# Hybrid layer: the next rows' transposes in the FFN moved from TensorE to VectorE blocks and device memory

## Chip, core and metric

The kernel runs on one core of one Trainium2 chip. The metric is device microseconds of a whole execution; lower is better. The core has TensorE (PE in the profile, with PEld for its weight loads), VectorE (DVE), ScalarE (ACT), GpSimd (POOL) and SyncE (SP), which here only issues DMAs. Engines wait for each other through semaphores alone.

## The reference, cut to what matters

Input `x` has 2 batches of 1024 rows of 512. Four sublayers follow each other, each added to `x`: a gated linear attention (A), an FFN (F1), a softmax attention (B) and the same FFN again (F2).

```python
def _qlinear(x, wq, scale):
    W = (wq - 128.0) * scale[:, None]
    return einsum('bsd,hd->bsh', x, W)
gate = silu(_qlinear(x, wq_gate, s_gate))            # 512 -> 1408
up   = _qlinear(x, wq_up, s_up)                      # 512 -> 1408
ffn  = _qlinear(gate * up, wq_down, s_down)          # 1408 -> 512
...
x = x + linear_attention(layernorm(x)); x = x + ffn(layernorm(x))
x = x + attention(layernorm(x));        x = x + ffn(layernorm(x))
```

## The kernel before, in words

The 2048 rows live in SBUF (`xres`), 16 tiles of 128 rows. An FFN block works on one batch (8 tiles), so there are four: F1,0 and F1,1, then B, then F2,0 and F2,1 (`blk` 0 to 3). A block has two parts.

The gate/up loop runs over `j`, the 11 slices of 128 hidden units. For each, TensorE makes seven partial products (pieces 1, 2, 7, 6, 4, 5, 3, each four matmuls of 512 columns), a scheme of seven block products on split 16-bit halves. They need the batch's normalised rows with the feature dimension on the partitions, as high and low parts of seven sums: `ab`, `12`, `34` and `2`. DVE, ACT and POOL combine the seven into `hid` and split it again. Piece 1 of `j = 0` waits for the low part of `ab`, pieces 6 and 5 for `12` low, and piece 7 for `34` low.

The down stage runs over `t`, the 8 row tiles: 11 matmuls of `hid_lo` and 11 of `hid_hi` per tile. ACT drains the low bank (`y_low`, L1233), DVE adds the high bank (`yt`, L1882), POOL scales (`yt`, L925), DVE adds to `xres` (`add_y`, L1801). The banks of `down_lo` are 6 and 2 in turn, of `down_hi` 5 and 7.

The next set of rows is prepared inside the block. A set is 8 tiles, handled as four pairs `i`. `x_stats` gives a row tile's mean and variance, `x_normalise` writes both tiles of a pair to `xn`, and TensorE turns them (`turn_x`, L2169: four 128x128 transposes for each tile, against an identity) into two PSUM banks. ACT copies the first bank to `x_first` (L1014) and makes the high parts (L1021, L1024); DVE makes `x_mid` by two subtractions (`x_second`, L1484 and L1487) and a low part (L1489); POOL makes `x_last` (`x_sums`, L753 and L755), `x_ab_low` (L761) and `x_12_low` (L767); ACT makes the high parts of `12` and `34` (L1028, L1037); DVE the low part of `34` (L1499 or L1496). Statistics are taken in the gate/up loop, one tile for each `j` from 2 to 9. The pairs are turned after `t` = 1, 3, 5 and 6 (`X_AFTER`), so their arithmetic stands between the `y` work of those tiles on each engine:

```python
X_AFTER = (1, 3, 5, 6)
NEXT_SET = (F1, B0, F3)          # made in blk 0, 1, 2
...
if blk < 3 and t in X_AFTER:     # TensorE, after tile t
    turn_x(NEXT_SET[blk], X_AFTER.index(t), 0)
    turn_x(NEXT_SET[blk], X_AFTER.index(t), 1)
```

The order on every engine is the order in which the code is written; nothing is reordered. The sets F0, B1 and F2 are made in the A and B stages in the same way, and `turn_x` serves those too.

Of the kernel before, what the change touches and what calls it, by code (L numbers as in the profile page):

```python
# [5 lines left out]
F32 = mybir.dt.float32  # L6
# [4 lines left out]
ALU = mybir.AluOpType  # L11
# [3 lines left out]
P = 128  # L15
# [34 lines left out]


# [6 lines left out]
def ffn_uses(**more):  # L58
    uses = {0: 24, 1: 20, 2: 15, 3: 12, 4: 10, 5: 4, 6: 4, 7: 4}
    for name, n in more.items():  # L60
# [30 lines left out]
NEXT_SET = (F1, B0, F3)  # L91
BLOCK_SET = (F0, F1, F2, F3)
# [7 lines left out]
def hybrid_layer_kernel(nc, x, wq, wk, wv, w_ab, bq, bk, bv, b_ab,  # L100
# [104 lines left out]


# [18 lines left out]
    yt = at("yt", Z + 81920, 2 * D)  # L225
    y_low = [at("y_low0", Z + 102400, D), at("y_low1", Z + 69632, D)]
# [29 lines left out]
    cla_dram = nc.dram_tensor("cla_dram", [4 * 4 * HEADS, P], F32, kind="Internal").ap()  # L256

# [59 lines left out]
    cla_masked = sem("cla_masked")  # L317
    cla_minus_done = sem("cla_minus_done")
# [110 lines left out]
    def x_banks(q, i):  # L429
# [212 lines left out]
    with block as blk:  # L642

        @blk.sync
        def _(sp):
# [75 lines left out]
            for b in range(BATCHES):  # L721
                for t in range(BT - b):
# [11 lines left out]
        def _(pool):  # L734
# [12 lines left out]
            def x_sums(q, i):  # L747
# [5 lines left out]
                nc.gpsimd.tensor_tensor(x_last[v][:, 0:2 * P], x_mid[v][:, 2 * P:4 * P], x_first[v][:, 0:2 * P],  # L753
                                        ALU.subtract).then_inc(x_t34_done, 1)
                nc.gpsimd.tensor_tensor(x_last[v][:, 2 * P:4 * P], x_first[v][:, 2 * P:4 * P],  # L755
                                        x_mid[v][:, 2 * P:4 * P], ALU.subtract).then_inc(x_t34_done, 1)

            def x_ab_low(q, i):
                n, v = 4 * q + i, X_PLACE[q]
                pool.wait_ge(x_ab_hi, n + 1)  # L760
                nc.gpsimd.tensor_tensor(x_ab(q, i, 1), four(x_first[v][:, :]), x_ab(q, i, 0),  # L761
                                        ALU.subtract).then_inc(x_ab_lo, 1)
# [234 lines left out]
        def _(act):  # L997
# [18 lines left out]
            def x_row_highs(q, i):  # L1016

                phase, b, first, second = x_banks(q, i)
                v = X_PLACE[q]
# [154 lines left out]
            def ffn(phase, b, extra):  # L1174
# [51 lines left out]
                for t in range(BT):  # L1226
# [247 lines left out]

# [1165 lines left out]
```

## Time and profile before

| | us |
|---|---|
| median of 3 runs (955.46 to 956.33) | 955.51 |
| the profiled execution | 955.11 |
| its span, first to last instruction | 953.4 |
| PE busy | 940.5 (99%) |
| DVE busy | 611.0 (64%) |
| POOL busy | 477.3 (50%) |
| ACT busy | 460.5 (48%) |

Busy time is the union of an engine's instructions over the span. The granted TensorE clock was 1.000 throughout, that is 2.4 GHz. Matmuls overlap in the records: one of 512 columns shows 0.38 us, though the next starts 0.22 us after it, so lengths of PE are read from the distance of starts. Some matmul records are missing. SP issues no DMA between 254 and 815 us.

### The profile page before, as it was taken

The numbers are of one execution on the slowest core, as the hardware profiler recorded it, in microseconds if no ns is written. First come the engines' busy times: TensorE is split into PE (matmuls) and PEld (weight loads), VectorE is DVE, ScalarE is ACT, GpSimd is POOL, SyncE is SP. The second block draws the span as 40 slices with busy tenths as digits, with TensorE's granted clock in tenths as the row PEclk, the third lists the DMA queues.
The fourth block names the chain that finished last, engine by engine and source line by source line (L and its number), as shares of the span: only waits on it lengthen the run. The fifth ranks groups of instructions, "written<-read, shape, count | busy, mean of one in ns | idle before, by whom it ended". The sixth has DMA issues, their size and how long they took to land.

```text
span 953.4 us, 13294 instructions
## 1 busy us (share of the span) xinstructions
PE 940.5 (99%) x4736; PEld 535.4 (56%) x4755; DVE 611.0 (64%) x1132; ACT 460.5 (48%) x918; POOL 477.3 (50%) x487
## 2 busy tenths in 40 slices
PE   7999999999999999999999999999999999999998
PEld 4888988888644444444444455445455444544444
DVE  7555647859678586776755466445575676766544
ACT  4443334356676535664533454323454665456631
POOL 5433424477276676666830043304233566665574
PEclk9999999999999999999999999999999999999999
DMA  9501300024200000000000000000000000110001
GB/s 319 178 3 34 133 23 23 2 89 145 105 17 1 1 1 1 1 1 1 1 1 1 1 1 1 1 1 1 1 0 1 1 0 1 45 45 1 1 22 69
DMA packets 14882, 30.31 MB, mean 32 GB/s; under 512 B 2080, under 2 KB 2400, under 8 KB 14816
## 3 DMA queue, kind: packets, MB, share of 16 engines
q1 hardware_dynamic: 14816, 29.45, 8.9%
q8 instruction: 39, 0.64, 0.3%
q14 instruction: 27, 0.22, 0.1%
HBM read 25.22 MB, written 4.23 MB: 31 GB/s over the span
## 4 chain that ended last, share of the span: by engine, by line
PE 93%; DVE 2%; ACT 1%; POOL 1%; DMA 1%; SPq 1%; issue 1%; DVEq 0%; POOLq 0%
PE psum L2120 54%; PE psum L2367 14%; PE psum L2369 14%; PE psum L2507 7%; PE psum L2169 2%; PE psum L2518 1%; DMA bq_col<-bq 1%; PE psum L2254 1%; PE psum L2158 1%; ACT probs L1347 0%; DVE xb_lo L2025 0%; ACT xb_hi L1353 0%; POOL wvT_lo L940 0%; POOL wo_lo L943 0%; SPq L652 0%
## 5 line engine op out<-in xcount | busy, mean ns | idle before, releaser
L882 POOL TENSOR_TENSOR hid<-hid,hid_hi 128x512 f32<-128x512 f32 x88 | 102.6, 1166 | 101.6 <-DVE hid_hi L1795 101.6
L2367 PE MATMUL psum<-xf,w_gu 128*128 128x512 f16 x352 | 133.8, 380 | 0.0
L2367 PE MATMUL psum<-xf,w_s 128*128 128x512 f16 x264 | 100.0, 379 | 0.6 <-DVE up L1768 0.4
L2369 PE MATMUL psum<-xf,w_gu 128*128 128x512 f16 x264 | 100.1, 379 | 0.0
L1209 ACT ACTIVATE hid_lo<-hid 128x512 f16<-128x512 f32 x88 | 55.0, 625 | 33.1 <-POOL hid L882 33.1
L878 POOL TENSOR_TENSOR hid<-up,gate 128x512 f32<-128x512 f32 x44 | 56.0, 1272 | 23.7 <-ACT gate L1204 23.7
L2369 PE MATMUL psum<-xq,w_s 128*128 128x512 f16 x176 | 66.7, 379 | 0.0
L2367 PEld LDWEIGHTS psum<-xf,w_gu 128*128 128x128 f16 x352 | 34.3, 97 | 53.9 <-ACT acc L1194 15.5
L1204 ACT ACTIVATE gate<-gate,sg_xs 128x512 f32<-128x512 f32 x44 | 31.7, 721 | 65.6 <-DVE gate L1778 65.6
L744 POOL TENSOR_TENSOR xrstd<-xvar,minus_half 128x1 f32<-128x1 f32 x48 | 25.5, 547 | 59.2 <-DVE xvar L1466 59.2
L1795 DVE TENSOR_SCALAR hid_hi<-hid 128x512 f16<-128x512 f32 x88 | 39.1, 445 | 19.4 <-POOL hid L878 17.9
L1760 DVE TENSOR_TENSOR gate<-psum,acc 128x512 f32<-128x512 f32 x44 | 30.4, 692 | 32.6 <-ACT acc L1182 22.4
L2120 PE MATMUL psum<-wd_b,hid_hi 128*128 128x512 bf16 (+1 forms) x192 | 47.3, 372 | 0.5
L925 POOL TENSOR_TENSOR yt<-yt,sd_rows 128x512 f32<-128x512 f32 x24 | 37.9, 1582 | 19.9 <-DVE yt L1882 19.9
L753 POOL TENSOR_TENSOR x_last<-x_mid,x_first 128x256 f32<-128x256 f32 x24 | 17.5, 727 | 60.5 <-DVE x_mid L1487 60.1
L2120 PE MATMUL psum<-wd_b,hid_lo 128*128 128x512 bf16 x184 | 46.1, 379 | 0.2
L2367 PEld LDWEIGHTS psum<-xf,w_s 128*128 128x128 f16 x264 | 25.9, 98 | 34.9 <-issue 3.8
L1778 DVE TENSOR_TENSOR gate<-psum,acc 128x512 f32<-128x512 f32 x44 | 30.3, 690 | 21.2 <-PE psum L2369 21.0
L2369 PEld LDWEIGHTS psum<-xf,w_gu 128*128 128x128 f16 x264 | 25.8, 98 | 31.0
L1342 ACT ACTIVATE probs<-psum 128x512 f32<-128x512 f32 x32 | 19.1, 597 | 48.3 <-PE psum L2507 48.3
L1787 DVE SCALAR_TENSOR_TENSOR hid<-psum,su_c,gate 128x512 f32<-128x512 f32 x44 | 33.0, 750 | 12.8 <-PE psum L2369 12.8
L1768 DVE SCALAR_TENSOR_TENSOR up<-psum,su_c,acc 128x512 f32<-128x512 f32 x44 | 33.0, 749 | 12.3 <-POOL hid L878 8.9
(314 smaller groups left out, 2560.6 us busy)
## 6 DMA issues: line engine op xcount, KB each, us to landing
cla_wide<-cla_dram SPq DMA_DIRECT2D x16, 256.0 KB, 3.4
out<-xres SPq DMA_DIRECT2D x15, 256.0 KB, 2.0
xres<-x SPq DMA_DIRECT2D x3, 1024.0 KB, 13.0
codes_gu<-gateT SPq DMA_DIRECT2D x1, 2816.0 KB, 11.7
codes_gu<-upT SPq DMA_DIRECT2D x1, 2816.0 KB, 10.8
codes_da<-downT SPq DMA_DIRECT2D x1, 1536.0 KB, 7.0
codes_db<-downT SPq DMA_DIRECT2D x1, 1280.0 KB, 11.4
xres<-x SPq DMA_DIRECT2D x4, 256.0 KB, 3.4
```

What stands on the lines that cost most here:

```text
L878: nc.gpsimd.tensor_tensor(hid2[:, :], up2[:, :], gate2[:, :], ALU.mult).then_inc(hid2_done, 1)
L882: nc.gpsimd.tensor_tensor(hid[:, :], hid[:, :], hid_part(hid_hi, j, half), ALU.subtract).then_inc(rest_done, 1)
L925: nc.gpsimd.tensor_tensor(cols(yt, t % 2), cols(yt, t % 2), sd_rows[:, :], ALU.mult).then_inc(y_scaled, 1)
L1204: nc.scalar.activation(gate2[:, :], gate2[:, :], ACT.Silu, scale=sg_xs[:, j:j + 1]).then_inc(silu2_done, 1)
L1209: nc.scalar.activation(hid_part(hid_lo, j, half), hid[:, :], ACT.Copy, scale=LO).then_inc(lo_done, 1)
L1768: nc.vector.scalar_tensor_tensor(out=up2[:, :], in0=bank(3 + j % 2), scalar=su_c[:, j:j + 1], in1=acc3[:, :], op0=ALU.mult, op1=ALU.add).t ...
L1787: nc.vector.scalar_tensor_tensor(out=hid1[:, :], in0=bank(j % 2), scalar=su_c[:, j:j + 1], in1=cols(gate1, j % 2), op0=ALU.mult, op1=ALU.m ...
L1795: nc.vector.tensor_scalar(hid_part(hid_hi, j, half), hid[:, :], ROUND, -ROUND, ALU.add, ALU.add).then_inc(hi_done, 1)
L2120: return nc.tensor.matmul(out, lhsT, rhs, start=start, stop=stop)
L2367: nc.tensor.matmul(bank(use[0]), w, x_operand(piece, k, False), start=start and k == 0, stop=False, skip_group_check=not start)
L2369: last = nc.tensor.matmul(bank(use[0]), w, x_operand(piece, k, True), start=False, stop=k == 1, skip_group_check=not start)
L2507: last = nc.tensor.matmul(bank(use[0]), l, r, start=start and k == 0 and j == 0, stop=k == 1 and j == 2, skip_group_check=not start)
```

## The change

For the three sets that are made in FFN blocks, TensorE's transposes are gone. DVE normalises both tiles of a pair into one buffer of 1024 columns and turns it in place in 32x32 blocks. SP writes the blocks to a buffer in device memory with four DMAs, one for each group of 32 partitions, and reads them back with four more, so that they arrive in `turned` in SBUF, fully transposed. Each DMA moves 128 KB in pieces of 128 bytes. ACT's copy to `x_first` is gone, and ACT, DVE and POOL read `turned` where they read PSUM or `x_first`.

The statistics now stand at `j` = 1 (three tiles) and 2 to 6; the rows of pairs 0 and 1 and their blocks at `j` = 7 to 12; those of pair 2 ahead of `t` = 0; those of pair 3 after `t` = 2. The arithmetic of the pairs stays at `t` = 1, 3, 5, 6.

```diff
+STATS_AT = {1: (0, 1, 2), 2: (3,), 3: (4,), 4: (5,), 5: (6,), 6: (7,)}
+ROW_AT = {7: 0, 8: 1, 10: 2, 11: 3}
+BLOCKS_AT = {9: 0, 12: 1}
+BLOCKS_AFTER = {2: 3}
...
-          ("F1", 0, ffn_uses(b0=2, b1=2, b3=2, b4=2)),
+          ("F1", 0, ffn_uses()),
...
+    xn_pair = [xn, yt, xn, at("xn_pair3", Z + 77824, 2 * D)]
...
+            def blocks_to_dram(q, *pairs):
+                for i in pairs:
+                    m = moved_n(q, i)
+                    sp.wait_ge(x_blocks_done, m + 1)
+                    src = xn_pair[i][:, :].rearrange("p (m j) -> p m j", j=SQ)
+                    for a in range(QUADS):
+                        sp.dma_start(blocks[m, a].rearrange("m (c i) j -> i (m c) j", c=QUADS),
+                                     src[a * SQ:(a + 1) * SQ, :, :]).then_inc(blocks_out[i % 2], 16)
+            def blocks_to_turned(q, *pairs):
+                for i in pairs:
+                    n, m = 4 * q + i, moved_n(q, i)
+                    if i < 2:
+                        phase, b = {F1: ("F1", 0), B0: ("F1", 1), F3: ("F2", 0)}[q]
+                        Use(sp, phase, b).read_out(delta(JT - 1, 1))
+                    else:
+                        sp.wait_ge(x_ab_lo, n - 1)
+                        sp.wait_ge(x_t34_done, 2 * n - 2)
+                        sp.wait_ge(x_2_lo_done, m - 1)
+                    sp.wait_ge(blocks_out[i % 2], moved_all(m))
+                    dst = turned[i % 2][:, :].rearrange("p (m a j) -> p m a j", a=QUADS, j=SQ)
+                    for a in range(QUADS):
+                        sp.dma_start(dst[:, :, a, :],
+                                     blocks[m, a].rearrange("m p j -> p m j")).then_inc(x_moved[i % 2], 16)
...
+            for q in MOVED:
+                blocks_to_dram(q, 0, 1)
+                blocks_to_turned(q, 0, 1)
+                blocks_to_dram(q, 2, 3)
+                blocks_to_turned(q, 2, 3)
+            store(0, *range(BT))
...
-                        x_copy(NEXT_SET[blk], i)
...
+            def x_pair_row(q, l):
+                i = l // 2
+                if i == 2 and l % 2 == 0:
+                    dve.wait_ge(blocks_out[0], moved_all(moved_n(q, 0)))
+                elif i == 3 and l % 2 == 0:
+                    dve.wait_ge(hid1_lo_done, JT * (MOVED.index(q) + 1))
+                    dve.wait_ge(hid2_lo_done, JT * (MOVED.index(q) + 1))
+                dve.wait_ge(ln_rstd_done, ln_n("X", q, l) + 1)
+                nc.vector.tensor_scalar(cols(xn_pair[i], l % 2), x_row(q, l), xmv[:, 2 * l:2 * l + 1],
+                                        xrstd[:, l:l + 1], ALU.subtract, ALU.mult).then_inc(ln_xn_done, 1)
+            def x_blocks(q, i):
+                dve.wait_ge(ln_xn_done, ln_n("X", q, 2 * i + 1) + 1)
+                nc.vector.transpose(xn_pair[i][:, :], xn_pair[i][:, :]).then_inc(x_blocks_done, 1)
...
+                if q in MOVED:
+                    dve.wait_ge(x_moved[m % 2], moved_all(m))
+                    t, first = turned[m % 2][:, D:2 * D], turned[m % 2][:, 0:D]
...
-                    if blk < 3 and 1 < j < 10:
-                        x_stats(NEXT_SET[blk], j - 2)
+                        for l in STATS_AT.get(j, ()):
+                            x_stats(NEXT_SET[blk], l)
+                        if j in ROW_AT:
+                            x_pair_row(NEXT_SET[blk], ROW_AT[j])
+                        if j in BLOCKS_AT:
+                            x_blocks(NEXT_SET[blk], BLOCKS_AT[j])
...
                 if blk < 3:
-                    x_normalise(NEXT_SET[blk], 0)
+                    x_rows_blocks(2)
                 def x_after(t):
...
-                        if i < 3:
-                            x_normalise(NEXT_SET[blk], i + 1)
+                    if blk < 3 and t in BLOCKS_AFTER:
+                        x_rows_blocks(BLOCKS_AFTER[t])
...
+                    if t == 0:
+                        dve.wait_ge(blocks_out[1], moved_all(moved_n(NEXT_SET[blk], 1)))
                     nc.vector.tensor_tensor(cols(yt, t % 2), bank(down_hi(t)[0]), y_low[t % 2][:, :],
...
-                    if blk < 3 and t in X_AFTER:
-                        turn_x(NEXT_SET[blk], X_AFTER.index(t), 0)
-                        turn_x(NEXT_SET[blk], X_AFTER.index(t), 1)
```

## Rows read from the trace of the kernel before

**Rows 1.** The page, its head and part 1.
```profile
span 953.4 us, 13294 instructions
PE 940.5 (99%) x4736; PEld 535.4 (56%) x4755; DVE 611.0 (64%) x1132; ACT 460.5 (48%) x918; POOL 477.3 (50%) x487
```

**Rows 2.** Timeline of PE in a down stage (start us, us, engine, line).
```profile
451.96 1.04 PE L2169 MATMUL psum<-ident,xn 128*128 128x128 f32 x8
452.84 1.24 PE L2120 MATMUL psum<-wd_a,hid_lo 128*128 128x512 bf16 x5
```

**Rows 3.** Timeline of PE where block F1,1 begins.
```profile
364.45 0.38 PE L2367 MATMUL psum<-xf,w_gu 128*128 128x512 f16 x1
```

**Rows 4.** Timeline of DVE in the down stage of block F1,0; brackets: idle before, releaser.
```profile
325.89 0.68 DVE L1778 TENSOR_TENSOR gate<-psum,acc 128x512 f32<-128x512 f32 x1
...
332.72 1.29 DVE L1882 TENSOR_TENSOR yt<-psum,y_low 128x512 f32<-128x512 f32 x2 [1.83 <-ACT y_low L1233]
...
341.88 1.75 DVE L1499 TENSOR_TENSOR xq<-x_last,xf 128x512 f16<-128x512 f32 x1
343.55 0.68 DVE L1882 TENSOR_TENSOR yt<-psum,y_low 128x512 f32<-128x512 f32 x1
...
345.20 0.42 DVE L1487 TENSOR_TENSOR x_mid<-psum,x_mid 128x256 f32<-128x256 f32 x1
...
353.41 0.69 DVE L1882 TENSOR_TENSOR yt<-psum,y_low 128x512 f32<-128x512 f32 x1 [1.26 <-PE psum L2120]
...
355.26 0.42 DVE L1487 TENSOR_TENSOR x_mid<-psum,x_mid 128x256 f32<-128x256 f32 x1
```

**Rows 5.** Timeline of POOL in the same stage.
```profile
354.18 1.65 POOL L925 TENSOR_TENSOR yt<-yt,sd_rows 128x512 f32<-128x512 f32 x1 [2.58 <-DVE yt L1882]
...
358.64 1.16 POOL L767 TENSOR_TENSOR xf<-x_mid,xf 128x512 f16<-128x512 f32 x1
359.80 1.67 POOL L925 TENSOR_TENSOR yt<-yt,sd_rows 128x512 f32<-128x512 f32 x1
361.43 1.61 POOL L761 TENSOR_TENSOR xf<-x_first,xf 128x512 f16<-128x512 f32 x1
...
364.49 1.15 POOL L767 TENSOR_TENSOR xf<-x_mid,xf 128x512 f16<-128x512 f32 x1
```

**Rows 6.** Timeline of ACT in the same stage.
```profile
347.54 0.63 ACT L1037 ACTIVATE xf<-x_last 128x512 f16<-128x512 f32 x1 [1.25 <-POOL x_last L755]
348.08 0.58 ACT L1233 ACTIVATE y_low<-psum 128x512 f32<-128x512 f32 x1
```

**Rows 7.** Timeline of DVE at the start of block F1,0.
```profile
258.10 1.41 DVE L1901 SCALAR_TENSOR_TENSOR wvo_lo<-psum,mids,wvo_hi 128x512 f16<-128x512 f32 x2 [1.11 <-ACT wvo_hi L1257]
...
262.24 0.75 DVE L1787 SCALAR_TENSOR_TENSOR hid<-psum,su_c,gate 128x512 f32<-128x512 f32 x1 [0.42 <-PE psum L2369]
...
264.65 0.69 DVE L1462 BATCH_NORM_STATS2 ln_bn<-xres 128x6 f32<-128x512 f32 x1
...
265.58 0.15 DVE L1466 TENSOR_SCALAR xvar<-xmv 128x1 f32<-128x1 f32 x1
266.00 0.69 DVE L1760 TENSOR_TENSOR gate<-psum,acc 128x512 f32<-128x512 f32 x1 [0.26 <-ACT acc L1182]
```

**Rows 8.** DVE by line: the rows' normalising, and the widest instruction (ns min/median/max).
```profile
L1472 DVE TENSOR_SCALAR xn<-xres,xmv,xrstd x48: 533/848/1385, 173.3 to 835.7; 128x512 f32<-128x512 f32 x48
...
L2017 DVE TENSOR_REDUCE smax<-probs x16: 1209/1219/1221, 510.8 to 718.5; 128x1 f32<-128x1024 f32 x16
```

**Rows 9.** DVE with one input in PSUM, and with both in SBUF, by line.
```profile
L1487 DVE TENSOR_TENSOR x_mid<-psum,x_mid x24: 424/424/426, 181.8 to 841.6; 128x256 f32<-128x256 f32 x24
...
L1499 DVE TENSOR_TENSOR xq<-x_last,xf x16: 676/784/1772, 198.3 to 846.1; 128x512 f16<-128x512 f32 x16
```

**Rows 10.** DMA issues: KB each, us from issue to landing.
```profile
out<-xres SPq DMA_DIRECT2D x15, 256.0 KB, 2.0
...
wab_raw<-w_ab SPq DMA_DIRECT2D x1, 32.0 KB, 4.1
```

More of the change, by code:

```diff
@@ L91 @@
 NEXT_SET = (F1, B0, F3)
+MOVED = NEXT_SET
 BLOCK_SET = (F0, F1, F2, F3)
@@ L204, in hybrid_layer_kernel @@
     X_PLACE = (0, 1, 1, 2, 3, 1)
+    turned = [at(f"turned{i}", Z + 61440 + 4096 * i, 2 * D) for i in range(2)]
     w_s = at("w_s", Z + 104448, 6 * HID, F16)
@@ L473, in x_2_cols, with x_first_of @@
         return slice(0, 4 * P) if q in (B0, B1) else slice(2 * P, 4 * P)
+    def x_first_of(q, i):
+        return turned[i % 2][:, 0:D] if q in MOVED else x_first[X_PLACE[q]][:, :]
     def x_pair(t, first, i):
@@ L1016, in x_row_highs @@
             def x_row_highs(q, i):
+                v = X_PLACE[q]
+                if q in MOVED:
+                    m = moved_n(q, i)
+                    act.wait_ge(x_moved[m % 2], moved_all(m))
+                    if m > 1:
+                        act.wait_ge(x_2_lo_done, m - 1)
+                    first, second = turned[m % 2][:, 0:D], turned[m % 2][:, D:2 * D]
+                    nc.scalar.activation(x_2(q, i, 0), second[:, x_2_cols(q)].rearrange("p (k n) -> p k n", n=P),
+                                         ACT.Copy).then_inc(x_b2_hi, 1)
+                    nc.scalar.activation(x_ab(q, i, 0), four(first), ACT.Copy).then_inc(x_ab_hi, 1)
+                    return
                 phase, b, first, second = x_banks(q, i)
-                v = X_PLACE[q]
                 Use(act, phase, b).full(second)
@@ L1473, in x_normalise @@
                                             xrstd[:, l:l + 1], ALU.subtract, ALU.mult).then_inc(ln_xn_done, 1)
-            def x_second(q, i):
-                phase, b, first, second = x_banks(q, i)
-                n, v, t = 4 * q + i, X_PLACE[q], bank(second[0])
-                Use(dve, phase, b).read_out(first)
+            def x_pair_row(q, l):
[11 more added lines that the diff above has]
+                nc.vector.transpose(xn_pair[i][:, :], xn_pair[i][:, :]).then_inc(x_blocks_done, 1)
+            def x_second(q, i):
+                n, v = 4 * q + i, X_PLACE[q]
+                if q in MOVED:
+                    m = moved_n(q, i)
+                    dve.wait_ge(x_moved[m % 2], moved_all(m))
+                    t, first = turned[m % 2][:, D:2 * D], turned[m % 2][:, 0:D]
+                    done = x_2_lo_done
+                else:
+                    phase, b, one, two = x_banks(q, i)
+                    Use(dve, phase, b).read_out(one)
+                    t, first, done = bank(two[0]), x_first[v][:, :], drained[two[0]]
                 dve.wait_ge(x_b2_hi, n + 1)
```

60 lines of the change are left out of this document (38 added, 22 removed).

## The prediction, made before the run

> **What bounds the kernel now.** Read the page's head first: TensorE is busy for 940.5 of 953.4 us, VectorE, the next, for 611.0 [rows 1]. So an instruction taken off TensorE is worth its whole length, as long as the other engines still deliver what it then asks for sooner. Next, PE's timeline in a down stage: the eight transposes of a pair start at 451.96 and the next matmul at 452.84 [rows 2], 0.88 us in which TensorE does nothing else. Last, how near the deliveries are to their deadline, at the seam from block F1,0 to F1,1. TensorE starts the new block at 364.45 [rows 3] and never waits there. GpSimd finishes the low part of `ab` for the last pair at 361.43 + 1.61 = 363.04 and of `12` at 364.49 + 1.15 = 365.64 [rows 5]. Piece 1 wants the first at 364.45, piece 6 the second eight matmuls later: four matmuls with hi and lo lie 0.216 us apart, so 8 x 0.216 = 1.73 and 366.18. The margins are 1.4 and 0.5 us. The reader is to see that the side engines have idle time on average and nearly none in this tail.
>
> **What is removed.** Three sets of four pairs, each 0.88 us: 12 x 0.88 = 10.5 us of TensorE. Without a new wait that is the gain, 3.5 us a block. ACT also loses its copies to `x_first`, which lie off the path. The next sections ask who is late when TensorE is 3.5 us sooner at the seam.
>
> **Statistics, three tiles at `j` = 1.** One tile takes from 264.65 to 265.58 + 0.15 = 265.73, 1.09 us with its gaps [rows 7]; three take 3.27. They stand ahead of `gate_first(1)` and so of `up_second(0)`, and piece 3 of slice 0 waits for the latter, since it reuses that bank. In block F1,0 VectorE is held until 258.10 + 1.41 = 259.51 by work of its first slice [rows 7]: 259.5 + 3.3 + 0.7 + 0.7 = 264.2 for the end of `up_second(0)`. TensorE comes to piece 3 four matmuls after piece 4, whose end released L1787 at 262.24 [rows 7]: about 263.0. A new wait of **1.2 us**, in this block alone; F2,0 has no such work, and F1,1 about comes out even.
>
> **Rows and blocks in the gate/up loop.** Where the statistics of one tile stand now, VectorE still idles 0.26 us [rows 7], so one row (0.53 us at least, 0.85 median [rows 8]) fits. A 32x32-block instruction on 1024 columns has no row. The nearest is one over 1024 columns out of SBUF, 1.22 us [rows 8]; from below two rows in one, 2 x 0.53 = 1.07; from above twice the nearest, 2.4, if it went through the data twice. I take 1.2. At `j` = 9 this costs nothing, at `j` = 12 it stands in the wait for the last `hid`. At 2.4 it would cost some tenths. Cost 0.
>
> **The path through device memory.** For a pair: four stores and four loads, 4 x 128 = 512 KB a way in 4096 pieces of 128 bytes. No row has such pieces. From below, by bytes: 256 KB land 2.0 us after issue [rows 10], so 512 KB in between that and twice that, 3.0. From above, by pieces: the load of `w_ab`, 32 KB in 512 pieces of 64 bytes, landed after 4.1 us with other loads ahead of it [rows 10]; eight times that is 33. I take 4.5 a way, near the lower end, because those 4.1 us hold a queue of 1 MB. The first deadline is that of pair 1: its blocks follow the last `gate_second`, which ends at 325.89 + 0.68 = 326.6, and are done near 328.4 (1.2 us, and some hold by GpSimd); `yt(0)`, at 332.7 [rows 4], now waits for its stores, since they read the `yt` buffer; 4.3 us, so I book 0.3 a block (**0.9 us**). Behind `yt(0)` on VectorE queue all sums of the stage. Pair 2 has 10 us for two ways after the blocks of pair 3, because SP writes pair 3 before it reads pair 2 back: at 4.5 a way it is hidden. SP is otherwise idle until 815; the eight stores of the output now queue behind the last set and have the 110 us of F2,1 as cover.
>
> The Trainium skill (DMA: Bandwidth & Descriptors, Specifications) wants at least 512 bytes a piece for line rate; below that it speaks of read-modify-write. No run here shows it for stores to device memory. It speaks for the upper half of that range and for the third case below.
>
> **The down stage, where the sum is decided.** After `t` = 2 VectorE now does two rows and the blocks of pair 3 ahead of `yt(3)`. The rows cost 2 x 0.53, the blocks 1.2, hand-overs 0.1: **2.4 us**. Before, `x_34_low(0)` ended at 343.63 and `yt(3)` followed at once, at 343.55 in the record, then the add and `x_second(1)`, whose second half ended at 345.62 [rows 4]. What the change takes out after `t` = 1 (`x_normalise`) was no part of this chain: there VectorE waits for ACT's `y_low(2)`, which stands behind the high part of `34` of the pair, as L1233 does behind L1037 at 347.54 and 348.08 [rows 6].
>
> A second term: `x_second` read PSUM and one SBUF tile, at 424 to 426 ns in every one of 24 cases; with both inputs in SBUF the same kind of instruction takes 676 to 1772 ns [rows 9], long when GpSimd is at work. After the change both inputs are in SBUF, and GpSimd's `yt` (1.65 us [rows 5]) starts just before it. The hold is between 0 and 1.1 us a pair; I take 0.6.
>
> The Trainium skill (SBUF — State Buffer, Who interferes with whom) says that a VectorE instruction with two SBUF inputs and a GpSimd one that reads SBUF exclude each other for their whole length, while one input in PSUM is free of that. Rows 9 agree: 424 to 426 against up to 1772 ns. It would put the hold at its upper end.
>
> So `x_second(1)` ends 2.4 + 0.6 = 3.0 us late. VectorE idles 1.26 us ahead of `yt(5)` (L1882 at 353.41 [rows 4]), which takes back as much: 1.7; `x_second(2)` adds 0.6: it ends 2.3 us after its 355.68 [rows 4]. From there GpSimd works without a gap, through 359.80 and 361.43 [rows 5], so nothing is taken back: `ab` low of the last pair at 363.04 + 2.3 = 365.3, and `12` low, with half a hold more for `x_second(3)` (0.4), at 365.64 + 2.7 = 368.3. TensorE, ready at 364.45 - 3.5 = 360.95, waits for `ab`, does eight matmuls, and waits again for `12`: piece 6 at 368.4 and not 366.2. Against before the seam is **2.2 us later** in F1,0 and F2,0. Block F1,1 leads into the attention, which asks at once for `ab` alone: 365.3 against 364.45, **0.9 us later**. With no hold these are 0.65 and -0.3, with the full hold 3.6 and 1.9.
>
> **The sum.** 2 x 2.2 + 0.9 + 1.2 + 0.9 = 7.4 us, the 10.5 us of transposes already in it (each block is compared by the clock times of before). Span 953.4 + 7.4 = 960.8; what lies around the span, 1.7 us, stays: 962.5 for the profiled execution. That execution took 955.11, 0.4 under the median of 955.51, so **962.9** for the median. Its own range, from no hold and stores in time (1.3 - 0.3 + 1.2 = 2.2) to full hold (7.2 + 1.9 + 1.2 + 0.9 = 11.2): 957.7 to 966.7.
>
> **The rivals.** *Faster: the side engines keep up.* If `x_second(1)` ends less than about 1 us late (a short block instruction, or GpSimd out of the way), the saving shows. GpSimd's gapless run is then the limit: from `yt` at 354.18 to `ab` low it is 8.9 us, to `12` low 11.5 [rows 5]. TensorE's fifth tile ends 2 x 0.88 earlier than before, so that run starts at 352.4 and ends at 361.3 and 363.9, against 360.95 and 362.7: waits of 0.35 and 1.2. Blocks: -2.3, -2.3, -3.15, and +1.2 for the statistics: -6.5, so 949.0. For it speaks that the three side engines have 36% to 52% of the span free; against it that the 2.4 us stand ahead of a chain with only 1.26 us of idle time.
>
> *Slower by the DMAs.* From about 5 us a way the transfers decide. At 8 us `yt(0)` is 3.7 us late instead of 0.3, and pair 2 a further 1.5: 3 x 4.9 more, 977.6. For it speaks the bound from above, against it the bound from below.
>
> *No change:* the terms cancel (no hold, and `y_low` sooner than I place it): 955.5.
>
> **How the numbers follow.** Forecast 0.50, side engines keep up 0.25, DMAs decide 0.18, cancelled 0.07. A measurement of this kernel can tell 0.2% (1.9 us) from no change. Faster 0.25, same 0.07, slower 0.68. The range of 8 in 10 takes in most of the faster case and the DMA case up to its price: 947 to 979.
>
> **What would show it.** The transposes of L2169 fall from 192 to 96. PE waits at three seams: about 4.4 us for `xf` or `xb_lo` of L761 each, another 1.3 for L767 at two of them, and 1.2 us for L1768 near 263 us; a bank wait for `y_low` near `t` = 6 may stand in for a part. The subtractions of `x_second` spread from 0.42 to 1.5 us. The block instruction shows 1.1 to 1.3 us. Each `turned` load lands ahead of its reader. The prediction is wrong if PE passes the seams without waits, or if DVE's longest waits are on `turned` or on `blocks`.

## The result, and the profile after

The changed kernel is slower: 965.43 us median against 955.65 of the kernel before beside it, ratio 1.0095 [1.0079, 1.0112]. One of the four executions took 2508.56 us and is left out of the ratio; the other three took 964.41, 964.75 and 966.12 us, and their median, 964.75, is what the ratio and every gain against "after" below are counted from. The profiled one took 964.75 us with a span of 963.0, 9.6 us above that of before. The forecast was 962.9, slower.

The page's head and part 1 of the kernel after, which answer to [rows 1]:

```profile
span 963.0 us, 13201 instructions
PE 935.6 (97%) x4643; PEld 524.6 (54%) x4659; DVE 624.3 (65%) x1144; ACT 454.7 (47%) x906; POOL 477.1 (50%) x487
```

TensorE is busy for less time than before, in a longer span. The records of the transposes (line, engine, count, ns min/median/max) fell from 192 to 96:

```profile
L2276 PE MATMUL psum<-ident,xn x96: 270/273/327, 175.2 to 729.7; 128*128 128x128 f32 x96
```

What TensorE waits for, after (total us, times, longest), with the first matmul behind the wait for `up`:

```profile
PE psum L2474 <- POOL xf L825: 7.0, 2, 3.5
PE psum L2227 <- POOL xb_lo L825: 4.2, 1, 4.2
...
PE psum L2474 <- ACT acc L1256: 1.6, 2, 0.8
PE psum L2474 <- DVE up L1864: 1.3, 2, 0.9
```

```profile
264.08 0.38 PE L2474 MATMUL psum<-xf,w_s 128*128 128x512 f16 x1 [0.88 <-DVE up L1864]
```

L825 is `ab` low (L761 before): the seams out of F1,0 and F2,0, 3.5 us each, and out of F1,1 into B, 4.2. L1864 is `up` (L1768 before), in the first block, which stands behind the statistics. Before, only one wait of 0.4 us for `up` stood in this list. TensorE at the first seam, after:

```profile
366.05 0.61 PE L2474 MATMUL psum<-xf,w_gu 128*128 128x512 f16 x1 [3.51 <-POOL xf L825]
366.45 0.63 PE L2476 MATMUL psum<-xf,w_gu 128*128 128x512 f16 x1
...
368.98 0.38 PE L2476 MATMUL psum<-xf,w_gu 128*128 128x512 f16 x1
370.15 0.38 PE L2474 MATMUL psum<-xf,w_s 128*128 128x512 f16 x1 [0.79 <-ACT acc L1256]
```

Block F1,1 started at 364.45 before [rows 3] and now at 366.05. Then something that no step foresaw: the next starts lie 0.40 to 0.43 us apart and not 0.216. Windows of the same trace (us; busy us and count of each engine; granted clock; DMA share; GB/s), over the wait and the matmuls behind it at this seam, and over the matmuls behind the wait at the seam into B:

```profile
362.50:366.00 3.50, 0.04 (x1) 0.00 (x0) 3.37 (x3) 0.50 (x2) 3.50 (x3) 0.93 0.00 0
366.10:369.30 3.20, 3.20 (x8) 0.98 (x8) 2.14 (x5) 1.04 (x2) 2.48 (x3) 0.56 0.00 0
...
478.90:482.50 3.60, 3.60 (x11) 1.40 (x12) 2.29 (x6) 1.32 (x3) 3.04 (x3) 0.63 0.00 0
```

Behind each of these waits, of 3.5 to 4.2 us, TensorE runs at the lower level, 1.2 GHz, for some 3 us. The seam into B before (first row) and after:

```profile
473.58 0.38 PE L2120 MATMUL psum<-xb_hi,g_hi 128*128 128x512 f16 x1
```

```profile
478.89 0.59 PE L2227 MATMUL psum<-xb_hi,g_hi 128*128 128x512 f16 x1 [4.23 <-POOL xb_lo L825]
...
481.71 0.38 PE L2227 MATMUL psum<-xb_lo,g_hi 128*128 128x512 f16 x1
```

VectorE and GpSimd in the down stage of F1,0, after, to be laid beside [rows 4, 5]:

```profile
327.70 1.23 DVE L1562 STREAM_TRANSPOSE yt<-yt 128x1024 f32<-128x1024 f32 x1
...
333.91 1.29 DVE L1989 TENSOR_TENSOR yt<-psum,y_low 128x512 f32<-128x512 f32 x2 [0.55 <-ACT y_low L1307]
...
341.36 0.69 DVE L1989 TENSOR_TENSOR yt<-psum,y_low 128x512 f32<-128x512 f32 x1 [2.50 <-issue]
...
344.50 0.99 DVE L1557 TENSOR_SCALAR xn_pair<-xres,xmv,xrstd 128x512 f32<-128x512 f32 x2
345.52 1.25 DVE L1562 STREAM_TRANSPOSE xn_pair<-xn_pair 128x1024 f32<-128x1024 f32 x1
...
347.86 1.49 DVE L1580 TENSOR_TENSOR x_mid<-turned 128x256 f32<-128x256 f32 x1
349.38 0.42 DVE L1583 TENSOR_TENSOR x_mid<-turned,x_mid 128x256 f32<-128x256 f32 x1
...
358.51 0.43 DVE L1583 TENSOR_TENSOR x_mid<-turned,x_mid 128x256 f32<-128x256 f32 x1
```

The 2.50 us are put down to "issue", which means that the profile shows no releaser; the instruction starts as ScalarE's first `y_low` of 340.69 ends (two of them in 1.12 us). GpSimd:

```profile
362.73 1.71 POOL L989 TENSOR_TENSOR yt<-yt,sd_rows 128x512 f32<-128x512 f32 x1
364.40 1.59 POOL L825 TENSOR_TENSOR xf<-turned,xf 128x512 f16<-128x512 f32 x1
366.82 0.84 POOL L818 TENSOR_TENSOR x_last<-x_mid,turned 128x256 f32<-128x256 f32 x1 [0.82 <-DVE x_mid L1583]
...
368.82 1.15 POOL L831 TENSOR_TENSOR xf<-x_mid,xf 128x512 f16<-128x512 f32 x1
```

`x_second(1)` ends at 349.38 + 0.42 = 349.80, 4.2 us later than before [rows 4], of which 1.2 came into the stage with the block. `ab` low of the last pair ends at 364.40 + 1.59 = 365.99, GpSimd having worked without a gap from the sums of pair 2 on; behind it GpSimd stands 0.82 us for VectorE. ScalarE, the first reader of `turned`, waits for the first pair's load:

```profile
336.42 0.42 ACT L1089 ACTIVATE xf<-turned 128x256 f16<-128x256 f32 x1 [2.11 <-DMA turned<-blocks]
```

It waits 1.59 us more for pair 2's, at 354.64. VectorE comes to these two pairs later than that, at 337.65 and 356.99. The DMAs, after (KB each, us from issue to landing):

```profile
turned<-blocks SPq DMA_DIRECT2D x48, 128.0 KB, 3.0
...
blocks<-xn SPq DMA_DIRECT2D x24, 128.0 KB, 2.9
```

The stores out of `yt` and `xn_pair` land after 2.6 us.

### The profile page after: what moved, and what is told of

Read it like the earlier page. It is cut to its first block, busy times and chain, and to the rows that moved or that the text cites. A ratio compares the mean times of both kernels' runs of the same rounds, so it can differ in the third digit from the quotient of the medians.

```text
span 963.0 us, 13201 instructions
## 1 busy us (share of the span) xinstructions
PE 935.6 (97%) x4643; PEld 524.6 (54%) x4659; DVE 624.3 (65%) x1144; ACT 454.7 (47%) x906; POOL 477.1 (50%) x487
## 4 chain that ended last, share of the span: by engine, by line
PE 77%; DVE 8%; issue 5%; POOL 3%; ACT 3%; SPq 2%; DMA 2%; DVEq 0%; ACTq 0%; POOLq 0%
PE psum L2227 42%; PE psum L2474 13%; PE psum L2476 12%; PE psum L2611 7%; DVE x_mid L1580 1%; PE psum L2622 1%; DVE xres L1897 1%; DMA turned<-blocks 1%; PE psum L2276 1%; DMA bq_col<-bq 1%; DVE xq L1595 1%; PE psum L2361 1%; DVE yt L1989 1%; SPq L754 1%; DVE x_mid L1583 1%
## 5 line engine op out<-in xcount | busy, mean ns | idle before, releaser
L2474 PE MATMUL psum<-xf,w_gu 128*128 128x512 f16 x352 | 135.6, 385 | 7.1 <-POOL xf L825 7.0
L2476 PE MATMUL psum<-xf,w_gu 128*128 128x512 f16 x264 | 101.6, 385 | 0.0
L2227 PE MATMUL psum<-wd_a,hid_hi 128*128 128x512 bf16 (+1 forms) x165 | 39.9, 373 | 0.2
L1864 DVE SCALAR_TENSOR_TENSOR up<-psum,su_c,acc 128x512 f32<-128x512 f32 x44 | 32.9, 749 | 9.1 <-POOL hid L942 7.6
```

The lines of the kernel that those rows point to most:

```text
L1864: nc.vector.scalar_tensor_tensor(out=up2[:, :], in0=bank(3 + j % 2), scalar=su_c[:, j:j + 1], in1=acc3[:, :], op0=ALU.mult, op1=ALU.add).t ...
L2227: return nc.tensor.matmul(out, lhsT, rhs, start=start, stop=stop)
L2474: nc.tensor.matmul(bank(use[0]), w, x_operand(piece, k, False), start=start and k == 0, stop=False, skip_group_check=not start)
L2476: last = nc.tensor.matmul(bank(use[0]), w, x_operand(piece, k, True), start=False, stop=k == 1, skip_group_check=not start)
```

## The experiments

The times of the kernels, each against runs of the kernel before on the same chip (955.5 to 955.8 us):

| kernel | median us | ratio [95%] | profiled span, clock |
|---|---|---|---|
| after | 965.43 (964.75 of three) | 1.0095 [1.0079, 1.0112] | 963.0, 0.995 |
| e1 statistics one for each `j` | 965.73 | 1.0108 [1.0088, 1.0128] | 966.6, 0.989 |
| e2 pair 3's rows after `t` = 1 | 960.96 | 1.0055 [1.0040, 1.0070] | 959.2, 0.996 |
| e3 plain DMAs | 967.51 | 1.0134 [1.0117, 1.0151] | 962.6, 0.995 |
| e4 split ahead of `add_y` | 962.92 | 1.0074 [1.0057, 1.0092] | 961.0, 0.996 |
| e5 = e1, e2 and e4 | 959.85 | 1.0041 [1.0026, 1.0055] | 957.0, 0.996 |
| e6 filler on TensorE | 966.88 | 1.0123 [1.0103, 1.0142] | 965.2, 1.000 |
| e7 = e5, pairs after 1, 2, 4, 5 | 959.26 | 1.0037 [1.0025, 1.0050] | 958.7, 0.998 |
| e8 = after, pairs after 1, 2, 4, 5 | 960.11 | 1.0048 [1.0033, 1.0062] | 957.9, 1.000 |
| e9 = e7 with plain DMAs | 957.61 | 1.0018 [1.0006, 1.0030] | 954.9, 1.000 |
| e10 = e7, `y_low` first | 957.41 | 1.0018 [1.0006, 1.0031] | 955.5, 0.998 |
| e11 = after, `y_low` first | 964.03 | 1.0088 [1.0073, 1.0103] | 963.4, 0.993 |
| e12 = e10, two orders | 953.62 | 0.9978 [0.9969, 0.9987] | 951.8, 0.998 |

The intervals of e1, e4, e6 and e11 overlap with that of after. Those of e9 and e10 overlap with e7's, and e7's with those of e5 and e8. The profiled spans have some of their difference ahead of all that is changed here: TensorE is 1.1 us later in e6 than in after at the first FFN block.

**Is it TensorE's work, or the side engines?** e6 gives TensorE the work back, as matmuls into a free bank:

```diff
+                    if blk < 3 and t in X_AFTER:
+                        use = down_lo(t + 1)
+                        u.free(use)
+                        for _ in range(4):
+                            mm(bank(use[0]), hid_hi[:, t * P:(t + 1) * P], w_down(0), True, True)
```

> The changed kernel with four matmuls of 512 columns (0.86 us) put back on TensorE after t = 1, 3, 5 and 6 of the first three blocks, in the place of the transposes; their result is overwritten, so only TensorE's time is tested. My theory: TensorE waits at each seam for longer than the 3.5 us that this adds, so the whole stays within 1 us or falls by up to 2 where the clock drop behind a wait goes; waits for the low part of ab fall from 3.7 and 4.4 us to about 0.2 and 0.9. If TensorE were the bound, 10.4 us are added.

48 matmuls of 0.216 us are 10.4 us, and the median is 2.1 us above that of after, with intervals that overlap; up to 1 us was expected. TensorE's waits in e6:

```profile
PE psum L2474 <- ACT acc L1256: 4.4, 2, 2.2
...
PE psum L2227 <- POOL xb_lo L825: 2.1, 1, 2.1
...
PE psum L2474 <- POOL xf L825: 1.0, 1, 1.0
```

The work went into the waits: for `ab` low 4.2 us at the seam into B became 2.1, and 7.0 at the other two 1.0, of which a part comes back ahead of piece 6: 4.4 us against 1.6 in after, put down to ScalarE's drain (L1256). `12` low ends 0.04 us before that drain, at 372.01, and the trace can't tell the two apart there. So TensorE is not what sets the time of these stages. The granted clock is 1.000, with no slow stretch, where after has three; one of them cost 1.3 us (below). So the removed work is worth 2 us of its 10.4 here, or 3 to 4 without the clock, which is an estimate from these numbers.

**Is it the DMAs?** e3 has one plain DMA a way and pair, in rows of 4 KB; the blocks are not put in their transposed places.

```diff
+                    sp.dma_start(blocks[m].rearrange("a m p j -> (a m p j)").rearrange("(p n) -> p n", p=P),
+                                 xn_pair[i][:, :]).then_inc(blocks_out[i % 2], 16)
...
+                    sp.dma_start(turned[i % 2][:, :], blocks[m].rearrange("a m p j -> (a m p j)")
+                                 .rearrange("(p n) -> p n", p=P)).then_inc(x_moved[i % 2], 16)
```

> The changed kernel with each pair written by one plain DMA of 4 KB rows and read back by one, in place of four and four with pieces of 128 bytes: the blocks are not put in place, so this part of the computation is left out, while every wait and every other instruction stays. It bounds what the small pieces and the eight issues cost. My theory: every load lands before its reader has anything to wait for but VectorE, so less than 1 us changes. Theory of the transfers: most of the 9.8 us goes.

Nothing was gained: the span is 962.6 against 963.0, with the same 7.0 and 4.2 us of waits for L825. The median is even higher. Its executions lie between 964.34 and 970.54; the two slowest, 967.85 and 970.54, have a granted clock of 0.989, the others one of 0.995, as after. 967.17 among the latter stays unexplained.

**Which part of the side engines' work?** e1, e2 and e4 each take one out of the way; e5 is all three. e4 moves the low part of `34` ahead of `add_y` together with the split.

```diff
-STATS_AT = {1: (0, 1, 2), 2: (3,), 3: (4,), 4: (5,), 5: (6,), 6: (7,)}
+STATS_AT = {j: (j - 1,) for j in range(1, 9)}          # e1, e5
-BLOCKS_AFTER = {2: 3}
+BLOCKS_AFTER = {1: 3}                                  # e2, e5
...
+                    if blk < 3 and t - 1 in X_AFTER and (t < BT - 1 or blk == 1):     # e4, e5
+                        x_34_low(NEXT_SET[blk], X_AFTER.index(t - 1))
+                    if blk < 3 and t in X_AFTER:
+                        x_second(NEXT_SET[blk], X_AFTER.index(t))
                     if t > 0:
                         add_y(blk, t - 1)
-                    if blk < 3 and t - 1 in X_AFTER and (t < BT - 1 or blk == 1):
-                        x_34_low(NEXT_SET[blk], X_AFTER.index(t - 1))
-                    x_after(t)
+                    if blk < 3 and t in BLOCKS_AFTER:
+                        x_rows_blocks(BLOCKS_AFTER[t])
```

> The changed kernel with its statistics one tile for each j from 1 to 8, where three stood at j = 1. My theory: the new wait of TensorE near 264 us (1.05 us ahead of L2474, piece 3 of slice 0 in F1,0) goes, and with it 1.0 to 1.3 us of the whole, about 963.9 at a median of 965; the waits at the three seams stay as they are. If the seams absorbed the wait, or if it had another cause, nothing changes.

> The changed kernel with rows and blocks of pair 3 after t = 1 and not after t = 2. There VectorE idles 2.50 us ahead of yt(2), and the three instructions take 2.35 us. My theory (the chain from x_second(1) on is late by what stands ahead of yt(3)): all later work of the stage moves 2.35 us earlier, the waits of TensorE for the low part of ab fall from 3.7 and 4.4 us to about 1.3 to 2, the whole by 7 us or, if the slow clock behind the waits also goes, by up to 9: 956 to 958. Theory of the transfers: pair 3 is written and read back earlier, but pair 2 was late for other reasons; no change beyond 1 us. Theory of the hold alone (two inputs in SBUF): the hold stays, no more than 1 us.

> The changed kernel with x_second placed ahead of the add to xres (add_y) of the tile before, right behind yt(t). Its first subtraction then starts before GpSimd's yt instruction does. My theory: the first subtraction shows 0.42 us and not 1.49, and ends 1.1 + 0.7 us earlier at pairs 0 to 2; the chain gains 3 us or more a block until TensorE's own pace or GpSimd's gapless run binds: 8 to 12 us in all, 953 to 957, and GpSimd's yt of these tiles is longer by up to 0.4 us. If only the rows and blocks after t = 2 count and the hold doesn't, 2 us at most.

> Statistics one for each j, pair 3 after t = 1, and x_second ahead of add_y, together. My theory: GpSimd's gapless run behind yt(5) is then the limit, with waits at the seams of 0.3 to 1.3 us; the rival of the prediction in which the side engines keep up was worked out at -6.5 us with the wait for the statistics, so without it and with a shorter tail 945 to 949. If the gains of the three don't add (one chain, one slack), no better than the best of them alone, 953 to 957.

e1 removed the wait near 264 us (the only one left for L1864 is 0.4 us), and gained nothing in the median. In its profiled execution F1,1 starts 1.1 us sooner than in after, but behind the seams the clock stayed low for longer: 0.51 over 5.7 us behind the seam into B, and behind the first seam:

```profile
365.00:372.40 7.40, 6.45 (x17) 2.06 (x18) 5.42 (x11) 3.06 (x5) 4.38 (x4) 0.54 0.01 2
```

Two of its four executions, 967.12 and 968.37, have a granted clock of 0.989. The other two have after's 0.995 and took 964.27 and 964.33, against 964.41 to 966.12: at the same clock some tenths of the 1.2 us arrive.

e2 gained 3.8 us, the largest of the three and about half of what was expected (956 to 958). Its waits for `ab` low fell as expected, from 3.5 and 4.2 us to 1.7 and 2.7, but the wait ahead of piece 6 rose from 0.8 to 2.2 at two seams. e4 gained 1.8 us, not clear of the noise, where 8 to 12 were expected, and e5 4.9 where 16 to 20 were. Each of these was computed along one chain, and another stands close behind. In e5 TensorE waited for L825 in two seams 4.8 us and in the third 3.6.

**Is it the place of the last pair?** Once nothing ties the pairs to TensorE's order, they can be split after `t` = 1, 2, 4 and 5; the last pair's ScalarE and GpSimd work then takes the form of the others', and SP stores and loads pair 2 before it stores pair 3. e8 is this alone, e7 this on e5, e9 is e7 with the DMAs of e3.

```diff
-X_AFTER = (1, 3, 5, 6)
+X_AFTER = (1, 2, 4, 5)
...
-                blocks_to_dram(q, 2, 3)
-                blocks_to_turned(q, 2, 3)
+                for i in (2, 3):
+                    blocks_to_dram(q, i)
+                    blocks_to_turned(q, i)
```

> The kernel after with all of e5_all_three, and the pairs split after t=1, 2, 4 and 5 in place of 1, 3, 5 and 6 (SyncE's order is then store 2, load 2, store 3, load 3, and the last pair's split is in the same order as the others'). In e5 the last pair's chain (row highs at 360.07 on ScalarE, its ab low behind the scaling of y(6) on GpSimd until 364.21) still ended behind TensorE, which waited 2.3, 3.75 and 2.3 us and then ran some matmuls at half the clock. Theory: it is only the place of the last pair that makes the seams; one tile (5.4 us) earlier it ends before TensorE's last matmul of the stage, and waits and slow stretches go together: the span of after, 963.0, less about 6.0, 5.9 and 6.0 at the three seams and 1.05 for the statistics, 944, so 946 us (944 to 950). Rival 1: the data is late for the earlier places (pair 3's load lands at about 352 to 355, its split would begin at 354.5), ScalarE then waits and holds y_low: 950 to 956 and a wait on the DMAs on ScalarE. Rival 2: the side engines are full from t=4 to t=6 and the wait moves to TensorE's down tiles (banks not drained): about 958, as e5.

> The kernel after with the places alone: pairs split after t=1, 2, 4 and 5, SyncE's order store 2, load 2, store 3, load 3; statistics, pair 3's rows and the order on VectorE as in after. Theory (the place of the last pair makes the seams): 947 to 951 us, since the rows of pair 3 still stand behind t=2. Rival 1 (data late): pair 3's rows are only ready at 347 and its load lands at about 355.5, so this one is 3 us or more slower than e7. Rival 2 (side engines full): about 962 to 965.

> e7 with one plain DMA (rows of 4 KB) each way per pair in place of the four stores and four loads of 128-byte pieces; this leaves out the transposition of the blocks among each other, so the numbers that come out are not the reference's. Theory: as e7 within 1.5 us, since the data has landed before it is used. Rival 1 (data late for the earlier places): 3 us or more faster than e7.

e8 gained 4.6 us, about as much as e5, and e7, 5.5, hardly more. ScalarE in e7 shows who hands whom on (L1107 is the 34 high, L1303 `y_low`, L1098 the 12 high), then VectorE:

```profile
356.91 0.63 ACT L1107 ACTIVATE xf<-x_last 128x512 f16<-128x512 f32 x1 [1.42 <-POOL x_last L821]
357.45 0.58 ACT L1303 ACTIVATE y_low<-psum 128x512 f32<-128x512 f32 x1
...
361.57 0.63 ACT L1098 ACTIVATE xf<-x_mid 128x512 f16<-128x512 f32 x1 [2.71 <-DVE x_mid L1573]
363.62 0.63 ACT L1107 ACTIVATE xf<-x_last 128x512 f16<-128x512 f32 x1 [1.42 <-POOL x_last L821]
364.16 1.07 ACT L1303 ACTIVATE y_low<-psum 128x512 f32<-128x512 f32 x2
```

```profile
358.12 0.69 DVE L1978 TENSOR_TENSOR yt<-psum,y_low 128x512 f32<-128x512 f32 x1 [1.82 <-ACT y_low L1303]
...
364.83 0.69 DVE L1978 TENSOR_TENSOR yt<-psum,y_low 128x512 f32<-128x512 f32 x1 [1.82 <-ACT y_low L1303]
```

A tile with a pair goes round in 364.83 - 358.12 = 6.7 us: `y_low`, `yt`, the split, GpSimd's sums, 34 high, and only then the next `y_low`. The expectation set TensorE's tile at 5.4 us against that; its timeline in after, two starts that are four tiles apart, makes it 19.00 / 4 = 4.75:

```profile
333.88 1.25 PE L2227 MATMUL psum<-wd_a,hid_lo 128*128 128x512 bf16 x5
...
352.88 1.24 PE L2227 MATMUL psum<-wd_a,hid_lo 128*128 128x512 bf16 x5
```

So a tile with a pair is 2 us behind TensorE, and only the tiles without one catch up. The expectations of 947 to 951 for e8 and 944 to 950 for e7 were missed: the place gave about a third of it. e9 is 1.65 us below e7, with intervals that overlap. There the load of the first pair does reach the chain: in e7 ScalarE waits 2.21 us for it and VectorE 1.83 us for ScalarE ahead of the first split, in e9 neither waits. Most of that is lost again in the round, so that of the transfers 1.65 us at most are visible, and only in this order.

**Is it that round?** e10 (on e7) and e11 (on after) let ScalarE copy `y_low` of the next tile before the 34 high:

```diff
+                    if blk < 3 and t - 1 in X_AFTER:
+                        x_34_high(NEXT_SET[blk], X_AFTER.index(t - 1))
                     if blk < 3 and t in X_AFTER:
-                        x_highs(NEXT_SET[blk], i)
-                        x_34_high(NEXT_SET[blk], i)
+                        x_highs(NEXT_SET[blk], X_AFTER.index(t))
```

> The kernel e7 with one order changed: ScalarE copies y_low(t+1) before the 34 high of the pair split after t, not behind it. In e7 the last pair was split one tile earlier, and yet its ab low ended at 364.70: ScalarE's queue stood at the 12 high and 34 high of a pair (357.45 for y_low of t=5, 364.16 for y_low of t=6, each right behind a 34 high), VectorE waited 1.82 us for it before each yt, and so the tiles went round VectorE, GpSimd and ScalarE in 6.7 us with a pair, where TensorE needs 5.4. Theory: this round (y_low, yt, second rows, GpSimd's sums, 34 high, y_low), not the work of any engine nor the place of the last pair, sets the down stage of the kernel after. With y_low ahead the yt of t=3, 5 and 6 come about 1.8 us earlier each, the wait of 1.0 to 1.6 us for a bank and the 1.5 to 2.2 us at the seams go, and with them the slow stretches: 958.7 of e7 less 3 x 4 to 3 x 5, about 945, so 945 to 950 us. Rival (the engines are full or GpSimd's port holds VectorE, so the order is worth nothing): 957 to 960. Second rival (late loads): as the first, with a wait on the DMAs on ScalarE ahead of a y_low.

> The kernel after with the one order changed: ScalarE copies y_low(t+1) before the 34 high of the pair split after t (pairs 0 to 2; the last pair's is behind y_low of t=7 already). Theory: in after y_low of t=4 came at 351.98 behind the 34 high of pair 1 (348.08 in before) and VectorE's yt stood 2.50 us for it three times a stage; with y_low ahead the last pair's chain begins 2 to 3 us earlier and the seam waits of 3.7, 4.4 and 3.7 shrink to 1 to 1.5, of the slow stretches half at most: 954 to 959 us. Rival (no round, only work): 964 to 966.

By these two, mostly not. The idle time of VectorE ahead of `yt` went as expected (three times 2.50 us in after, and 0.90 in e11), but e11 gained 0.7 us on after and e10 1.85 on e7, neither clear of the noise, where 6 to 11 and 9 to 14 were expected. e10's VectorE, by line (busy us, mean ns, idle before), in its down stage of F1,0:

```profile
L1887 DVE TENSOR_TENSOR xres<-xres,yt 128x512 f32<-128x512 f32 x6 | 8.1, 1358 | 0.0
...
L1570 DVE TENSOR_TENSOR x_mid<-turned 128x256 f32<-128x256 f32 x4 | 3.8, 940 | 3.1 <-ACT xf L1085 1.7 <-POOL xf L832 1.2
```

The adds to `xres` take 1358 ns on average, against 1007 ns in the same stage of the kernel before (six of them, 6.0 us): VectorE, no longer idle, is now held there while GpSimd works. In part the hold only moved: the low part of `34` takes 895 ns on average in e10 and 1750 in after. Windows of the same 29 us of the down stage, in the kernel before, after, and e10:

```profile
334.00:363.00 29.00, 28.84 (x145) 14.69 (x147) 23.30 (x33) 11.69 (x22) 23.77 (x20) 1.00 0.00 1
```

```profile
334.00:363.00 29.00, 28.43 (x130) 12.72 (x130) 20.56 (x27) 10.60 (x21) 20.63 (x19) 1.00 0.67 104
```

```profile
334.00:363.00 29.00, 27.64 (x129) 12.35 (x128) 23.83 (x30) 11.36 (x22) 25.25 (x22) 1.00 0.63 97
```

GpSimd (the fifth pair of numbers after the length) is at 25.3 of 29 us in e10, VectorE at 23.8. Two engines at 82% and 87% that feed each other in turn have little left. That this is why the order was worth so little is argued, and e12 limits it: its VectorE and GpSimd are as busy in these 29 us (24.4 and 25.1), and it is 3.8 us faster than e10.

**What order serves TensorE?** e12 (on e10) makes pair 3's rows and blocks in the longest idle stretch left on VectorE, 1.7 us ahead of the first split, and the last pair's `ab` low before its sums. In that stretch ScalarE waits for the first pair's load (2.13 us in e10). SyncE's order is back to store 2, store 3, load 2, load 3:

```diff
+                    if blk < 3 and t in BLOCKS_AFTER:
+                        x_rows_blocks(BLOCKS_AFTER[t])
                     if blk < 3 and t in X_AFTER:
                         x_second(NEXT_SET[blk], X_AFTER.index(t))
                     if t > 0:
                         add_y(blk, t - 1)
-                    if blk < 3 and t in BLOCKS_AFTER:
-                        x_rows_blocks(BLOCKS_AFTER[t])
...
+                        if i == 3:
+                            x_ab_low(NEXT_SET[blk], i)
                         x_sums(NEXT_SET[blk], i)
-                        x_ab_low(NEXT_SET[blk], i)
+                        if i < 3:
+                            x_ab_low(NEXT_SET[blk], i)
                         x_12_low(NEXT_SET[blk], i)
```

> The kernel e10 with two orders changed (and SyncE's back to store 2, store 3, load 2, load 3, which the first one asks for). One: VectorE makes the rows and blocks of pair 3 after yt(1) and ahead of the first pair's split, where it stood idle for 1.75 us until the first load had landed, in place of behind it. Two: GpSimd makes the last pair's ab low ahead of its two sums. e10 showed the stage with hardly any idle on VectorE (0.46 us and 1.22 us from 336 to 365), and GpSimd busy 25.3 of 29 us: a chain made of work, in which only work moved into an idle stretch, or work done in the order in which TensorE asks for it, helps. Theory: the first change brings the tiles forward by up to 1.75 us, the second makes ab low ready 2 us earlier, so that the waits of 1.5, 3.0 and 2.2 us at the seams and the half clock behind the second of them (1.7 us) go; the 1.2 us ahead of the gate sum (VectorE late with add_y and the 34 low) stay in part. 957.4 less 5 to 8: 949 to 953 us, below the kernel before. Rival (GpSimd is the bound, its work is the same in any order, so that only the 12 low comes later): 956 to 958. Second rival (the first pair's split, 1.7 us later, is what the tiles hang on): 958 or more.

953.62 us, ratio 0.9978 [0.9969, 0.9987]: the transposes off TensorE, and 2 us faster than the kernel before, 0.6 us above the range expected. The two orders were not tried one by one. TensorE's waits in e12:

```profile
PE psum L2468 <- ACT y_low L1305: 3.9, 2, 2.0
...
PE psum L2221 <- POOL xb_lo L825: 0.3, 1, 0.3
```

The waits for `ab` low are gone but for 0.3 us; what is left at the seams of F1,0 and F2,0 is the drain of the last tile (`y_low` of `t` = 7, behind the last pair's 34 high), 2 us each.

## Why the prediction was right, and where its terms were off

Its mechanism held: VectorE and GpSimd deliver the next rows later, and TensorE, without its transposes, waits for them at all three seams. The size came near in part by luck, as the sum below shows.

**The transposes** were worth a little less than the 10.5 us booked. The last matmuls of `t` = 1 in block F1,0, before and after:

```profile
331.82 0.81 PE L2120 MATMUL psum<-wd_b,hid_hi 128*128 128x512 bf16 x2
```

```profile
333.02 0.81 PE L2227 MATMUL psum<-wd_b,hid_hi 128*128 128x512 bf16 x2
```

From there to the point where TensorE is ready for the next block the stage took 364.45 - 331.82 = 32.6 us before and 362.37 - 333.02 = 29.35 after: 3.3 us, or 9.8 in all if the other two blocks do the same. (362.37 is the start at 366.05 less the 3.68 us that it lies beyond the usual distance.)

**Statistics**, 1.2 us: right, by 1.05 to 1.2. TensorE stood 0.88 us for `up` near 264 (L1864 above), its start there came 1.05 us late, and the block is 1.2 us behind at 322. e1 confirms that the place of the statistics makes it: the wait went. That the whole did not get shorter by it is in the profiled execution the clock's doing; in the two executions at after's clock it is not shown where the rest went.

**The stores**, 0.9 us: not there, though their length was nearly right. Those of pair 1 take 2.24 us to issue and the last lands 2.6 us after its issue, 2.24 x 3/4 + 2.6 = 4.3 us (4.5 booked), so at about 333.2. `yt(0)` came at 333.91, released by `y_low`, 1.2 us later than before and so no later than its block. The blocks were done at 328.93 and not at 328.4 + 1.2 = 329.6, which is the 0.3 us that was booked and more.

**The loads** took longer than the 4.5 us booked: a group of eight took 8.01 and 5.96 us to issue and a load lands 3.0 us after its issue, so four of them take 8.01 x 3/8 + 3.0 = 6.0 or 5.96 x 3/8 + 3.0 = 5.2 us. Not each landed ahead of its reader, as was forecast: ScalarE waited 2.11 and 1.59 us. It cost nothing here, since VectorE came to the same pairs later still, and e3, where these waits are gone, has the same waits at the seams. The Trainium skill (DMA: Bandwidth & Descriptors, Specifications) was cited for its at least 512 bytes a piece for line rate; pieces of 128 bytes cost nothing that e3 could see, and at most 1.65 us in e7's order.

**The seams of F1,0 and F2,0**, 2.2 us each: 2.7. In the block's own time, 1.2 us late, `x_second(1)` ends 4.2 - 1.2 = 3.0 late (predicted 3.0), and `x_second(2)`, at 358.94, 3.3 - 1.2 = 2.1 (predicted 2.3) against 355.68 [rows 4]. Behind both numbers stand errors that cancel: rows and blocks took 0.99 + 1.25 us (predicted 2.4 with hand-overs), and `yt(5)`, at 355.79 against 353.41, is 1.2 late where 1.7 were expected, but the hold of pairs 1 and 2 was 1.07 and not 0.6: `x_second`'s first subtraction took 1.49 us where 0.42 is its free time. That is the upper end, where the Trainium skill (SBUF — State Buffer, Who interferes with whom) had put it, and the trace agrees. From there the tail went otherwise than told. `ab` low of the last pair, at 365.99, is 1.75 late in the block's own time (predicted 2.3), and `12` low 3.1 (predicted 2.7): behind `ab` low GpSimd does not work without a gap but stands 0.82 us for `x_second(3)`. `12` low came at 369.97 (predicted 369.5 with the 1.2), and piece 6 at 370.15 against 366.25: 3.9 - 1.2 = 2.7. The trace puts its wait down to ScalarE's drain (L1256), which ends 0.04 us after `12` low. In F2,0 the seam costs 2.7 as well (piece 6 at 854.82 against 845.24, the down stage before it 6.9 us late).

**The seam into B**, 0.9 us: 2.7, the term that was most mis-sized. The start itself was 1.4 us late (478.89 against 473.58, less the 3.9 by which the block was late already). But from there the clock was at half: seven starts to 481.71 took 2.82 us in place of 1.51, 1.3 us that nothing hid, since the attention asks for `ab` alone. No term of the prediction had the clock. At the other seams the slow matmuls ran while `12` low was waited for anyway. A last 0.3 us is spread over what follows, up to the down stage of F2,0.

**The sum** is 1.2 + 2 x 2.7 + 2.7 + 0.3 = 9.6 us against 7.4, and the span grew by 9.6. The time lies inside the likeliest case's own range, towards its slow end. The 0.9 us booked for stores that cost nothing made up for half of the 1.8 us that the seam into B cost beyond its term: luck.

**The rivals.** That the side engines keep up fell: they were late at every seam. That DMAs decide fell with e3. That the terms cancel fell with the ratio, whose interval starts at 1.0079. A rival that was missed is that the round over ScalarE, VectorE and GpSimd has its own length, longer than TensorE's tile once the transposes are gone; e7 showed it, and e10 and e11 that taking one hand-over out of it gives little, perhaps because two engines are nearly full. Where the 10.5 us went is thus told: into waits at the seams, and e6 put as much work back for 2.1 us.

Open: why an execution of e3 took 967.17 at after's clock, which of e12's two orders did it, and what part of the gains from e5 to e12 is the clock's, whose low stretches differ from one execution to the next.

## What to carry to other kernels

Taking work off the busiest engine pays only up to the next deadline of the others: read their margin at the seam (here 1.4 and 0.5 us) and not their share of the span. When a chain over three engines has become the bound, moving single links gave less than each chain computed alone; put work into an idle stretch, and make first what the waiting engine asks for first. A move that frees an order (the pairs were tied to TensorE's tiles) is worth re-planning that order at once: e8, three pairs moved by a tile and SyncE's order with them, gave 4.6 us.

## What the hardware did that was not expected

TensorE's granted clock fell to 1.2 GHz behind all three seam waits in after, for some 3 us each, and for up to 7 in e1 (0.54 over 7.4 us), but behind none in e6, e8 and e9, whose longest waits at a seam are 2.2, 2.6 and 2.0 us. The length of the wait does not settle it. Of the seam into B, the windows of e5, behind a wait of 3.6 us, and of e7, behind 2.0 us:

```profile
475.60:479.20 3.60, 3.55 (x17) 1.68 (x18) 3.01 (x5) 1.78 (x3) 3.44 (x4) 1.00 0.00 0
```

```profile
475.80:479.40 3.60, 3.50 (x9) 1.30 (x10) 3.47 (x4) 1.66 (x2) 2.64 (x2) 0.55 0.00 0
```

Seventeen matmuls in one, nine in the other. A wait can so cost more than its own length, as the 1.3 us at the seam into B did in after, which no count of instructions shows.

In-place turning in 32x32 blocks of 128x1024 took 1.23 to 1.25 us in all twelve cases of after, close to the 1.22 us of L2017 [rows 8], which goes over as many columns once. DMAs of 128-byte pieces landed in 2.6 to 3.0 us, but SyncE needs time to issue them. Its timeline, after (the second number is the whole group's length):

```profile
328.95 2.24 SPq L754 DMA_DIRECT2D blocks<-yt  x4
331.29 8.01 SPq L771 DMA_DIRECT2D turned<-blocks  x8
```

A store takes 0.56 us to issue and a load 0.73 to 1.0, so eight loads hold the queue for 5.8 to 8.0 us: longer than each of them flies.
